# Three instead of eight SBUF buffers for the streamed Toeplitz matrices of a long-convolution stage

## The reference, cut to what matters

```python
z = rmsnorm(u, pre_norm_w) @ in_proj_w.T          # then a 3-tap convolution, split in x2, x1, v
h = jnp.sum(residues[:, :, None] * jnp.exp(log_poles * t[None, None, :]), axis=1)
xv = x1 * v
yconv = jnp.fft.irfft(jnp.fft.rfft(xv, n=n) * jnp.fft.rfft(h, n=n)[None], n=n)[..., :Lc]
y = (yconv + xv * D_skip[None, :, None]) * x2
y = y.transpose(0, 2, 1) @ out_proj_w.T + u       # then the MLP, layer norms and the second network
```

## Time and profile before

| what | value |
|---|---|
| three runs | 1117.75 us median, 1116.7 to 1120.4 |
| the profiled execution | 1117.75 us, span 1116.0 us |
| phase A | about 0 to 198.9 us of the span |
| phase B | about 198.9 to 271.0 us |
| phase C | 271.0 us to the end |
| mean granted TensorE clock | 0.983 of full speed |

### The profile page before, as it was taken

The page is one execution under the profiler, slowest core; times in us unless marked ns, Lnnn a source line. Parts: engine busy times, 40 slices in busy tenths (PEclk is TensorE's granted clock), DMA queues, the critical chain, the costliest instruction groups (busy, mean ns, idle before and its releaser), DMA issues.

```text
span 1116.0 us, 25570 instructions
## 1 busy us (share of the span) xinstructions
PE 1052.6 (94%) x9280; PEld 1022.3 (92%) x9280; DVE 883.2 (79%) x2313; ACT 724.1 (65%) x1607; POOL 295.6 (26%) x560
## 2 busy tenths in 40 slices
PE   4999999896788999999999999989999999999996
PEld 4899999675778999999999999979999999999996
DVE  7998988673589788778888887898777888877874
ACT  6888887664565566666566666665665666666553
POOL 7676674540001211111121111111111211111121
PEclk9999999998898999999999999998999999999999
DMA  3337988994643234333333333442333333333000
GB/s 125 115 124 223 252 210 203 359 339 73 147 80 40 47 53 65 60 51 58 49 49 51 54 67 59 105 104 39 58 50 56 49 51 53 65 56 55 25 16 29
DMA packets 113246, 104.96 MB, mean 94 GB/s; under 512 B 7601, under 2 KB 104017, under 8 KB 112865
## 3 DMA queue, kind: packets, MB, share of 16 engines
q1 hardware_dynamic: 111952, 100.89, 41.5%
q0 software_dynamic: 672, 2.39, 0.6%
q10 hardware_dynamic: 496, 0.05, 0.0%
HBM read 77.84 MB, written 32.80 MB: 99 GB/s over the span
## 4 chain that ended last, share of the span: by engine, by line
PE 67%; DVE 7%; issue 4%; DMA 2%; ACT 1%; POOL 1%; SPq 0%; ACTq 0%; DVEq 0%; POOLq 0%
PE ps_ring L1406 35%; PE ps_w L1406 14%; PE ps_m L1406 9%; PE ps_o L1406 4%; PE ps_rt L1416 2%; PE ps_y L836 2%; PE ps_y L845 1%; DMA toep<-toep_scratch 1%; DVE base L1262 1%; DVE state L799 1%; POOL sc L1030 1%; PE ps_s L814 1%; DVE bn L1168 1%; PE ps_m L1452 1%; DMA base<-in_w 0%
## 5 line engine op out<-in xcount | busy, mean ns | idle before, releaser
L1030 POOL TENSOR_TENSOR sc<-sc,neg_half 128x2 f32<-128x2 f32 x128 | 95.3, 744 | 722.4 <-DVE sc L1361 432.6
L1090 ACT ACTIVATE gate<-ps_ring 128x256 f32<-128x256 f32 x192 | 73.0, 381 | 136.0 <-PE ps_ring L1406 134.1
L1406 PE MATMUL ps_ring<-mt_h,wl_h 128*128 128x256 f32 x640 | 130.3, 286 | 6.4 <-ACT mt_h L1157 6.4
L1406 PE MATMUL ps_ring<-mt_l,wl_h 128*128 128x256 f32 x640 | 130.1, 285 | 6.1 <-DVE mt_l L1180 6.1
L1111 ACT ACTIVATE hid<-ps_ring,b1s 128x256 f32<-128x256 f32 x256 | 113.6, 489 | 31.5 <-PE ps_w L1406 13.4
L1406 PE MATMUL ps_ring<-mt_h,wl_l 128*128 128x256 f32 x640 | 129.3, 284 | 0.0
L1180 DVE TENSOR_TENSOR ht_l<-hid,ht_h 128x256 fp32r<-128x256 f32 x256 | 103.3, 423 | 15.3 <-ACT ht_h L1115 9.5
L1406 PEld LDWEIGHTS ps_ring<-mt_h,wl_h 128*128 128x128 f32 x640 | 101.2, 195 | 7.7 <-ACT mt_h L1157 4.4
L1406 PEld LDWEIGHTS ps_ring<-mt_l,wl_h 128*128 128x128 f32 x640 | 100.6, 194 | 7.3 <-DVE mt_l L1180 7.3
L1406 PE MATMUL ps_ring<-xt_h,we_h 128*128 128x256 f32 x512 | 102.5, 281 | 2.4 <-DVE prod L1210 1.5
L1210 DVE TENSOR_TENSOR prod<-ps_ring,gate 128x256 f32<-128x256 f32 x192 | 80.9, 421 | 29.5 <-ACT gate L1090 24.8
(11 more groups left out here) (179 smaller groups left out, 2765.9 us busy)
## 6 DMA issues: line engine op xcount, KB each, us to landing
toep_scratch<-taps_scratch SPq DMA_DIRECT2D x30, 512.0 KB, 7.7
toep<-toep_scratch SPq DMA_DIRECT2D x30, 512.0 KB, 9.1
xa<-in_x SPq DMA_DIRECT2D x16, 512.0 KB, 4.7
x_scratch<-x2c SPq DMA_DIRECT2D x16, 512.0 KB, 3.7
x2s<-x_scratch SPq DMA_DIRECT2D x32, 256.0 KB, 6.9
xa_c<-in_x SPq DMA_DIRECT2D x32, 256.0 KB, 2.7
xb_c<-in_x SPq DMA_DIRECT2D x32, 256.0 KB, 2.7
out<-frow SPq DMA_DIRECT2D x32, 256.0 KB, 2.9
```

The source lines that it names most:

```text
L1030: nc.gpsimd.tensor_tensor(sc[:, to], sc[:, to], neg_half[:, 0, 0:CC], ALU.pow).then_inc(S[done], 1)
L1090: nc.scalar.activation(gate[rows_of, m % 2], ring[m % RING][rows_of, 0], ACT.Gelu_apprx_tanh).then_inc(S["gate_done"], 1)
L1406: mm = nc.tensor.matmul(out, lhs(a, kk), rhs(b, kk), start=(j == 0), stop=(closed and j == len(todo) - 1))
```

## The change

One constant of phase B changes: the number of buffers of `toep`. The tile shrinks from 32 KB to 12 KB per partition; `raw` and `post`, which are laid out behind it, move to lower addresses. The number of semaphores `toep_in` follows.

```diff
     to_end, ahead, own, later = (v[n] for n in "to_end ahead own later".split())
-    TOEPS, HALF = 8, P // 2
+    TOEPS, HALF = 3, P // 2
     PAIRS = GC // KB
     SEAM = GROUPS - 4
```

## The result

The changed kernel takes 1125.53 us (median of 8 runs, 1122.06 to 1128.4) against 1119.53 us for the kernel before (8 runs, 1116.7 to 1120.93) on the same chips: ratio 1.0058, 95% interval 1.0043 to 1.0074, so about 6.5 us slower (the two medians themselves are 6.0 apart). The forecast was +1.5 us. The profiled execution of the changed kernel happens to be a quick one, 1118.85 us, the lowest of its 31 executions on record (the others take 1120.9 to 1129.7), because its phase C is 5.7 us shorter than that of before; no other profile of this study shows such a phase C (they have 844 to 847 us from L1193 to the end, this one 839.3), and I have no reason for it. Phase B alone tells the change, and it is compared from the first L647 to the start of L1193: 277.78 - 199.30 = 78.5 us against 271.00 - 198.89 = 72.1, so +6.4.

What follows compares the result with a forecast made beforehand. TensorE, 94% busy, was taken to set the pace. Start 0, lpb 0.5 - 0.5, large load 0.6 - 0.6, steady state 0 and end +1.5 gave +1.5 us, from 1117.75 to 1119.3 us; range over the cases 1116.8 to 1124.5.

Steps and rivals of the forecast that it cites:

- The steady state: Phase B's matrix loads take 4.1 to 4.4 us with 4.93 us allowed, slack 0.5 to 0.8: cost 0.
- Where the two delays go: Phase B: delays of 0.5 us (lpb) and 0.6 (GpSimd's large load) vanish in scan holds at groups 11 and 18: net 0.
- The start: Phase B's first groups: the queue is still backed up, so group 5's matrix lands as before: cost 0.
- The end: End of phase B: gathers stand behind load 31 and x2s, so L1193 starts +1.5 us later (+0.5 to +2.7).
- A: Phase B: three buffers don't cover the load round trip; +6.6 us, 1124.4 us, at 5.5 us per load; chance 0.25.
- The point from which it decides: Phase B: a load costs time once it takes more than 4.93 us from issue to the product needing it.
- B: Phase B: hidden to the end, gathers timed by their issue and matrix 31 in time; +0.3 us at most, 1117.9; chance 0.13.
- C: Phase B: faster, as fewer queued matrices let weights and groups 4 and 5 land sooner; -1.5 us, 1116.3; chance 0.06.

Runs made afterwards that it cites:

- e15: Changed kernel (three buffers) with all phase B transfers left out but the matrices, x2s, the gathers and the small ones; ratio to the kernel before 1.0009.
- e16: e15 with eight buffers instead of three; ratio to the kernel before 0.9973.
- e6: Changed kernel without GpSimd's two later weight loads (256 KB of out_w, 640 KB of l3_w); ratio to the kernel before 1.0017.
- e1: Changed kernel with room for eight matrices, so all addresses of before, but only three buffers used; ratio to the kernel before 1.0059.
- e7: Changed kernel with the four 56 KB gathers moved to GpSimd's queue; ratio to the kernel before 1.0034.
- e11: Changed kernel with lpb loaded in four 256 KB pieces behind the matrices of groups 8 to 11; ratio to the kernel before 1.0044.
- e3: Changed kernel with four buffers instead of three; ratio to the kernel before 0.9999.
- e4: Changed kernel with five buffers instead of three; ratio to the kernel before 1.0002.
- e2: Changed kernel with two buffers instead of three; ratio to the kernel before 1.0192.
- e13: Changed kernel with lpb not loaded, ScalarE reading the first table again; ratio to the kernel before 1.0045.
- e14: Changed kernel with neither lpb nor GpSimd's two later weight loads; ratio to the kernel before 1.0016.

## Why the prediction was wrong

The forecast was +1.5 us and no change that can be measured; it came out at +6.5. The measured 1125.53 us lies above the range, which ended at 1124.5 and was counted from 1117.75, the median of the three runs then at hand. The steps from product to product divide the 6.4 us of phase B in the profile by the terms of the forecast: start +0.5 (forecast 0), the delays of groups 9 to 15 less the vanished holds by the scan +3.0 (forecast 0), the second half from group 22 on +1.9 (forecast 0), the end +1.0 (forecast 1.5).

**The steady state, forecast 0: half right.** The pace between holds is 2.02 us and 15 loads take 3.4 to 4.8 us. But the step read 4.1 to 4.4 us off four loads and took it for the bound of all. A slack of 0.5 us has to be set against the slowest load and not the usual one; 5.3 us stood in the earlier trace rows and was explained away by `x2s` (in the trace of before a 16 KB packet starts 1.5 us after that load's issue). With the matrices alone on the engines (e15, e16) three buffers still cost 3.4 to 4.0 us, of which the end is about 1.2. This step failed.

**Where the two delays go, forecast net 0: wrong, and by this profile the larger miss** (by e15 and e16 the two are about equal). The delays were mis-sized and the absorption came out far too small. lpb was to make group 9 late by 0.5: it did so by 1.3, and the load behind it, which the forecast had on time, by another 1.8. GpSimd's two late loads were to cost 0.6 in one place; the 256 KB one had been given nothing at all, and it is issued at 217.38, just before group 10's load, which takes 8.2 us. The large one met groups 13 and 14 (6.2 and 5.2 us) and not 15 to 17. Taken out together the two late loads give back 3.6 to 4.6 us (e6). The holds by VectorE's scan did vanish, 1.9 us, so the exchange is real: once TensorE is late, a scan stretched by GpSimd's split no longer holds it. But 1.9 us against 5.6 of matrix waits isn't a wash. The locked port of the Trainium skill's page (SBUF — State Buffer, section "SBUF: two separate sides") was the argument for it, and the trace agrees: a scan that starts later under a split still ends 0.55 us after it. But a lock can only take up a delay as long as the hold it had made.

**A term that wasn't there: the clock.** After a hold of 1.8 us TensorE's granted clock fell to the low level for about 3 us and two bundles took 1.3 us longer. Over all profiles with three buffers it fell during or just after eight holds of 1.73 to 3.91 us (as in e1 after 2.81) and not after two of 1.91 and 1.99 us (e7, e11), nor right after any of 1.54 or less.

**The start, forecast 0: nearly.** Group 5's matrix landed at 212.2 and not 211.2, because the queue did run low before its load was issued, and it was waited for 0.61 us; before, groups 4 and 5 together had waited 1.22. Another 0.8 us came from the low clock in the first bundle (1.97 instead of 1.09 us). That is in e3 and e4 as well, whose times equal before's, so it isn't the change's.

**The end, forecast +1.5: right in kind, +1.0 in size.** It was put down to the place of the gathers behind matrix 31. e7 shows that it is the collision and not the place: on another queue they slow matrix 31 by as much as they gain.

**The rivals.** A (slower, +6.6 us at a mean of 5.5 us per load, chance 0.25) has nearly the mechanism: loads overrun 4.93 us. That it has the size as well is luck. The mean of the 27 loads is 5.1 us and not 5.5, by which its formula gives 1.5 us and 3.0 with its end; what costs are twelve loads above the slack, some of them far above. The point from which it decides was right: e3 with 6.95 us allowed has no cost, e2 with 2.9 us allowed has the full cycle. B and C are out; every three-buffer kernel that moves all its bytes is slower. Their numbers were loose too: B's +0.3 us lies below the +0.5 that the forecast had as the lower end of its last term, and C's -1.5 doesn't follow from a third of 3.1 us less the end.

The 6.5 us in parts, as far as the runs divide them: 4.0 us stay when the matrices are alone on the engines (e15 against e16), for slow single loads and the end, and the other transfers add about 2.5. That is the only division with its own kernel of eight buffers. Among the kernels of three buffers the late weights give back 4.6 us (e6), and lpb 1.5 (e13, not clear of the measurement) or, once the late weights are out, 0.1 (e14 against e6). These don't add up with the 4.0, and how they divide the 2.5 stays open. What the slow loads of groups 22, 26 and 30 are due to is very likely the instruction fetch, by the table above, and not shown by a run.

## What to carry to other kernels

Size a ring of buffers by the slowest load that the stage will see, not by the quiet one: here 4.93 us allowed against a usual 4.3 lost 0.6%, and one buffer more (6.95 us) lost nothing, while four more than that gained nothing. A deep ring also lets the queue run ahead through a stretch in which other transfers fill the DMA engines; before cutting it, list every transfer of the stage, also those that nobody waits for. To price one transfer by leaving it out, leave it out of the kernel with the long ring as well; here that control is there for all transfers together and missing for each alone. And when a new wait is said to be taken up by an old one, it can be taken up only to the old one's length.

## What the hardware showed unasked

Small neighbours on another queue can nearly double a load: with 0.9 MB on GpSimd's queue the load of group 10 took 8.2 us, without it 5.6, and the usual load takes 4.3. A hold of TensorE of 1.8 us in a stretch at full clock was followed by about 3 us at half clock, so that it cost 3.1 us in all; most holds of such a length did so, not all. Packets of 16 KB of instructions go over DMA engines about every 8 us, and of the loads in the quiet half that had one start 1.5 to 3 us after their issue, 21 of 25 took over 4.93 us, against 1 of 73 that met none. Between two profiles of kernels that differ in addresses alone (the changed one and e1) the longest hold moved from group 10 to group 14.
